# A decoder kernel's first stage, the projection of x for latent attention: by groups of four batches, or by single batches with the next group made in between

## The chip, the cores and the metric

The kernel runs on one core of one Trainium2 chip. The metric is the device time of one execution in microseconds; three timed runs of the kernel before gave 3162.03, 3165.73 and 3168.84, median 3165.73.

## The reference

A decoder of two layers on x of 16 batches by 100 tokens by 512 features: latent attention, cross attention and a sign-quantised feed-forward in layer 0, attention, cross attention and a quantised feed-forward in layer 1, each with a residual sum and a layer norm behind it. The stage in question computes, for all 1600 tokens, what the latent attention needs:

```python
cq = h_t @ Wc + bc                      # 512 -> 128
q = (cq @ Wcq + bcq)                    # 128 -> 512
qr = _rope((cq @ Wqr + bqr))            # 128 -> 256
ckv = h_t @ Wckv + bckv                 # 512 -> 128
k = (ckv @ Wck + bck)                   # 128 -> 512
kr = _rope((h_t @ Wkr + bkr))           # 512 -> 256
v = (ckv @ Wv + bv)                     # 128 -> 512
```

The rotation is not in this stage. Each token's q, qr, k, kr and v leave as one row of 16 heads x 160 values (10 KB), with a few columns of padding between.

## The kernel before

The program is written engine by engine: for each stage there is a function for SyncE (which issues all DMAs), TensorE, ScalarE, VectorE and GpSimd, and semaphores between them. A stage's functions begin by waiting until the stores of the stage before have landed (`finish`, L210). The order of each engine is the order of the code; nothing is planned by a scheduler.

Matmuls are made with parts: an operand is split into a high part (ScalarE, `copy_hi`, L160) and a low part (VectorE, `sub_lo`, L163), and `mm3` (L166) adds three products on lines L168, L169 and L170. So every operand passes ScalarE, then VectorE, before TensorE can read it.

The stage `mla_project` (L594), written m1 in the tile names, works in 4 groups of 4 batches (400 tokens). `weights` (L229) loads seven weights through two landing buffers, `raw0` and `raw1`; a load waits until the low part of the weight before it in that buffer is made. Behind them SyncE issues eight small loads (`small_load`, L571: biases broadcast over 128 partitions, two columns, the padding), then x of the first group (L376, 100 partitions x 4 x 512). Per group TensorE turns x (16 transposes, L427, through three banks), waits for all high and low parts, makes the two features cq and ckv (24 matmuls of 400 columns), waits for their high and low parts, and projects batch by batch: q, qr, k, kr, v, 24 matmuls a batch, into five banks. VectorE adds the bias to each of the five outputs (L730) while it writes them to one of two row buffers, and SyncE stores each batch's rows (L652). A row buffer is written again when its store has landed. On all engines the groups are turns of a hardware loop (`Fori`).

`load_next` (L206) issues the first two weights of the next stage, `kv_and_attend`, as soon as their landing buffers are free; here it stands behind the loop of three groups, ahead of the last four stores.

## Time and profile before

| | |
|---|---|
| median of three timed runs | 3165.73 us (3162.03 to 3168.84) |
| the profiled execution's own time | 3160.35 us |
| its span | 3158.5 us |
| TensorE busy in the span | 2777.5 us, 88% |
| VectorE, ScalarE, GpSimd busy | 2065.2, 1676.1 and 1727.2 us |
| the stage in question | 0 to 162.0 us |

The span is the time between the first and the last instruction of the profiled execution. Each engine runs its instructions in order, so a wait in one delays all behind it on that engine. The granted clock of TensorE is given as a share of 2.4 GHz: 0.50 is 1.2 GHz. In names of tiles the buffer numbers are left out, so m1_x0 is written m_x. A DMA share is the mean busy share of the core's 16 DMA engines.

### The profile page before, as it was taken

How to read it: one execution, taken by the hardware profiler on the slowest of the kernel's cores; microseconds unless marked ns; L12 is line 12 of the kernel's file. 1: busy time of each engine (PE TensorE's matmuls, PEld its weight loads, DVE VectorE, ACT ScalarE, POOL GpSimd, SP SyncE). 2: the span in 40 equal slices, each digit the busy share in tenths (PEclk: the TensorE clock that was granted, in tenths of full speed). 3: DMA queues.
4: the chain of work that ended last, by engine and by line, in shares of the span. 5: the costliest groups of instructions: out<-in, count | busy, mean ns of one | idle time of the engine just before them, and what ended most of it. 6: DMA issues, size and time to landing. Idle time of an engine off the chain costs nothing. (4 is left out here: it accounts for less than half of the span.)

```text
span 3158.5 us, 48987 instructions
## 1 busy us (share of the span) xinstructions
PE 2777.5 (88%) x16162; PEld 2495.8 (79%) x16162; DVE 2065.2 (65%) x4090; ACT 1676.1 (53%) x4247; POOL 1727.2 (55%) x2145
## 2 busy tenths in 40 slices
PE   5789999964899999998599789999999997789998
PEld 4668888754788888886499778898888886669998
DVE  3467777743687888888446547677777777774334
ACT  1056666611788888776164355666656553443222
POOL 0057777700666766666154357888888786450000
PEclk9989999966999999998799889999999998889999
DMA  3545545434343333333321221321212111542101
GB/s 122 187 132 162 154 146 160 140 96 142 106 133 101 112 114 98 106 101 105 85 82 59 81 100 54 100 79 35 89 42 86 36 51 51 173 131 92 32 27 32
DMA packets 215374, 310.74 MB, mean 98 GB/s; under 512 B 47259, under 2 KB 112895, under 8 KB 213023
## 3 DMA queue, kind: packets, MB, share of 16 engines
q1 hardware_dynamic: 215134, 307.73, 31.1%
q8 instruction: 128, 2.10, 0.3%
q14 instruction: 112, 0.91, 0.1%
HBM read 211.30 MB, written 96.37 MB: 97 GB/s over the span
## 5 line engine op out<-in xcount | busy, mean ns | idle before, releaser
L925 POOL TENSOR_TENSOR mh_quant_d<-mh_quant_a,mh_quant_d 128x512 f32<-128x512 f32 x208 | 277.9, 1336 | 17.4
L1000 ACT ACTIVATE mh_quant_d<-mh_quant_d 128x512 f32<-128x512 f32 x256 | 159.8, 624 | 109.7 <-POOL mh_quant_d L925 109.4
L919 POOL TENSOR_SCALAR mh_quant_d<-mh_quant_a 128x512 f32<-128x512 f32 x208 | 132.9, 639 | 129.1 <-DVE mh_quant_err L903 81.3
L903 DVE TENSOR_REDUCE mh_quant_err<-mh_quant_d 128x8 f32<-128x512 f32 x256 | 173.6, 678 | 39.0 <-ACT mh_quant_d L1000 37.2
L1645 PE MATMUL bank<-ga_eT,ga_v 128*128 128x400 f32 (+1 forms) x384 | 169.9, 524 | 30.4 <-DVE ga_zl L1831 30.3
L1602 PE MATMUL bank<-ga_xt,ga_wqh 128*128 128x400 f32 x512 | 177.9, 410 | 1.6 <-DVE ga_xt L164 1.6
L2342 POOL TENSOR_TENSOR fq_var<-fq_mv,eps_ln 100x1 f32<-100x1 f32 x16 | 3.7, 229 | 315.5 <-DVE fq_mv L2285 315.5
L1371 POOL TENSOR_TENSOR kv_krs<-kv_kms,minus_half 128x4 f32<-128x4 f32 x48 | 50.0, 1042 | 230.0 <-DVE kv_kms L1359 228.7
L1795 ACT ACTIVATE ga_e<-ga_e,ga_nm 100x361 f32<-100x361 f32 x256 | 152.7, 597 | 38.5 <-DVE ga_nm L1890 37.0
L958 POOL TENSOR_TENSOR ga_quant_d<-ga_quant_a,ga_quant_near 128x512 f32<-128x512 f32 x128 | 165.2, 1291 | 13.5 <-DVE ga_quant_err L903 3.0
L1791 ACT ACTIVATE ga_e<-ga_e,ga_rs 100x361 f32<-100x361 f32 x256 | 152.6, 596 | 17.9 <-DVE ga_rs L1872 17.9
L1884 DVE SCALAR_TENSOR_TENSOR ga_e<-bank,ga_qrs,ga_mask 100x361 f32<-100x361 f32 x256 | 151.1, 590 | 14.3 <-PE bank L170 13.1
L1918 POOL TENSOR_TENSOR ga_qrs<-ga_qms,minus_half 100x4 f32<-100x4 f32 x64 | 68.3, 1068 | 168.3 <-DVE ga_qms L1825 168.3
L1774 ACT ACTIVATE ga_eT<-bank 128x300 f32<-128x300 f32 x256 | 106.4, 416 | 79.0 <-PE bank L1635 78.0
L923 POOL TENSOR_SCALAR mh_quant_d<-mh_quant_d 128x512 f32<-128x512 f32 x208 | 136.9, 658 | 17.2
L921 POOL TENSOR_SCALAR mh_quant_d<-mh_quant_d 128x512 f32<-128x512 f32 x208 | 132.9, 639 | 17.2
L1890 DVE TENSOR_REDUCE ga_nm<-ga_e 100x1 f32<-100x361 f32 x256 | 135.5, 529 | 6.7
L2731 ACT ACTIVATE mh_e<-mh_e,mh_nm 100x100 f32<-100x100 f32 x256 | 93.7, 367 | 86.2 <-DVE mh_nm L2846 86.2
L2302 DVE TENSOR_TENSOR fq_v<-fq_v 128x400 f32<-128x400 f32 x64 | 36.8, 575 | 136.6 <-ACT fq_v L2223 136.6
L1602 PEld LDWEIGHTS bank<-ga_xt,ga_wqh 128*128 128x128 f32 x512 | 97.4, 195 | 28.2 <-issue 2.0
L2223 ACT ACTIVATE fq_v<-bank 128x400 f32<-128x400 f32 x64 | 32.3, 505 | 163.8 <-PE bank L170 163.8
L168 PE MATMUL bank<-mh_zh,mh_woh 128*128 128x400 f32 x256 | 94.7, 370 | 25.6 <-DVE mh_acc L2805 16.5
(442 smaller groups left out, 10467.6 us busy)
## 6 DMA issues: line engine op xcount, KB each, us to landing
keys_turned<-kv_kt SPq DMA_DIRECT2D x16, 1448.0 KB
ga_kt<-keys_turned SPq DMA_DIRECT2D x64, 362.0 KB, 2.9
ga_xt<-x_turned SPq DMA_DIRECT2D x48, 400.0 KB, 4.9
mh_xt<-x_turned SPq DMA_DIRECT2D x48, 400.0 KB, 4.7
qkv<-m_rows SPq DMA_DIRECT2D x16, 1000.0 KB
kv_rows<-qkv SPq DMA_DIRECT2D x50, 320.0 KB, 3.3
raw<-x SPq DMA_DIRECT2D x64, 200.0 KB
kv_ctx<-in_ctx SPq DMA_DIRECT2D x32, 256.0 KB
```

The costliest lines, as they stand in the source:

```text
L903: nc.vector.tensor_reduce(self.of(self.err, i)[:, s, :], self.error(i, s), AX, ALU.add).then_inc(self.summed.sem, 1)
L919: nc.gpsimd.tensor_scalar(e, a[:], 1.0 / SHRINKS[s], MAGIC, ALU.mult, ALU.add).then_inc(made.sem, 1)
L923: nc.gpsimd.tensor_scalar(e, e, -MAGIC, SHRINKS[s], ALU.add, ALU.mult).then_inc(made.sem, 1)
L925: nc.gpsimd.tensor_tensor(e, a[:], e, ALU.subtract).then_inc(self.diff.sem, 1)
L958: nc.gpsimd.tensor_tensor(self.d[s % 2][:], a[:], near[:], ALU.subtract).then_inc(self.diff.sem, 1)
L1000: nc.scalar.activation(self.error(i, s), self.error(i, s), ACT.Square).then_inc(self.squared.sem, 1)
L1602: last = nc.tensor.matmul(ps, wq[c // 2][:, k, w_], xt[:, k, c % 2, :], start=n == 0, stop=n == 11, skip_group_check=True)
L1645: last = nc.tensor.matmul(z_bank[:, 0:N], v[m % 3][0:kk, c, :], eT[m % 2][0:kk, c, :], start=c == 0, stop=c == 2, skip_group_check=True)
L1791: nc.scalar.activation(E[o % 4][:, 0:S2], E[o % 4][:, 0:S2], ACT.Copy, scale=rs[o % 4][:])\
L1795: nc.scalar.activation(E[n % 4][:, 0:S2], E[n % 4][:, 0:S2], ACT.Exp, bias=nm[n % 4][:], accum_out=sm[n % 4][:]).then_inc(exped.sem, 1)
L1884: nc.vector.scalar_tensor_tensor(out=E[n % 4][:, 0:S2], in0=score_bank[n % 2][0:S, 0:S2], scalar=qrs[g % 2][:, hh, j:j + 1], in1=small["ma ...
L1890: nc.vector.tensor_reduce(nm[n % 4][:], E[n % 4][:, 0:S2], AX, ALU.max, negate=True).then_inc(maxed.sem, 1)
```

## The change

The stage is written anew as straight code, without loops. x is loaded by batches (100 partitions x 512) into four buffers; x0 and x1 are the first two DMAs of the program, ahead of Wc and Wckv, x2 and x3 come next, then the other weights. All seven weights have places of their own in the two landing buffers, so no load waits for another; they are split in four pieces instead of seven. The biases are loaded on 100 partitions, those of qr and kr as one tile behind the small loads.

TensorE turns one batch into one bank (4 transposes), two banks in all. Behind the projections of batches 0 and 1 of a group it turns two batches each of the next group, and behind that of batch 2 it makes the next group's features; batch 3 comes last. xh, xl, ch and cl are doubled. kr goes into the second half of qr's bank, so a batch has four outputs in four banks, and four adds. There are four row buffers. GpSimd writes the padding, VectorE did before. The next stage's two weights are issued ahead of the last two stores; before, ahead of the last four. In `weights` and in the cross attention the wait of a load for its landing buffer is now on the last reader that was noted instead of on a numbered one.

```diff
...
     def mla_project():
         ph, ctx, G = "m1", ExitStack(), 4
...
+        N, BG, XR, RR = G * S, B // G, 4, 4
+        quarter = lambda n: raw[n // 4][:, n % 4 * 512:(n % 4 + 1) * 512]
...
+        four = lambda a: a.rearrange("p (k n) -> p k n", k=KC)
+        landing = [[(four(quarter(0)), kview(t["L0_attn_Wc"])), (four(quarter(1)), kview(t["L0_attn_Wckv"]))],
+                   [(quarter(2), t["L0_attn_Wcq"]), (quarter(3)[:, 0:256], t["L0_attn_Wqr"])],
+                   [(quarter(4), t["L0_attn_Wck"]), (quarter(5), t["L0_attn_Wv"])],
+                   [(four(raw[1][:, 1024:2048]), kview(t["L0_attn_Wkr"]))]]
+        landed = [raw[0][:, 0:1024].rearrange("p (c k n) -> p c k n", c=2, k=KC), raw[0][:, 1024:1792],
+                  raw[1][:, 0:1024], four(raw[1][:, 1024:2048])]
+        parted = [wc, wq, wkv, wkr]
+        NW = len(parted)
         small, small_load, small_wait = small_loads(ph, ctx, [
...
+            ("pads", [S, 2, 2, PAD], F32, t["row_pads"].rearrange("n t s c -> t n s c")),
+            ("bcq", [S, 512], F32, row(t["L0_attn_bcq"], S)),
+            ("bck", [S, 512], F32, row(t["L0_attn_bck"], S)),
+            ("bv", [S, 512], F32, row(t["L0_attn_bv"], S))])
+        brr = sb(f"{ph}_brr", [S, 2, 256], F32, ctx)
+        x = [sb(f"{ph}_x{n}", [S, D], F32, ctx) for n in range(XR)]
+        xh, xl = ([sb(f"{ph}_x{s}{n}", [P, KC, N], F32R, ctx) for n in range(2)] for s in "hl")
+        ch, cl = ([sb(f"{ph}_c{s}{n}", [P, 2, N], F32R, ctx) for n in range(2)] for s in "hl")
+        rows = [sb(f"{ph}_rows{n}", [S, H, ROW], F32, ctx) for n in range(RR)]
+        x_bank, c_bank, out_bank = bank[0:2], bank[2:4], bank[4:8]
...
+        for slot in range(RAWS):
+            raw_read[slot].append((w_lo.sem, w_lo.upto(NW - 1)))
...
+        def turned_after(b_):
+            g, j = divmod(b_, G)
+            if g + 1 == BG:
+                return []
+            return [4 * (g + 1) + 2 * j, 4 * (g + 1) + 2 * j + 1] if j < 2 else []
+        def features_after(b_):
+            g, j = divmod(b_, G)
+            return g + 1 if j == 2 and g + 1 < BG else None
         def do_sp():
...
+            def load_x(e):
+                sp.dma_start(x[e % XR][:], rows_of(x0, e)).then_inc(x_in[e % XR].sem, 16)
+            def load_weight(n):
+                for to, src in landing[n]:
+                    sp.dma_start(to, src).then_inc(w_in[n].sem, 16)
+            load_x(0)
+            load_x(1)
+            load_weight(0)
+            load_x(2)
+            load_x(3)
+            for n in range(1, NW):
+                load_weight(n)
             small_load()
...
+            for n, name in enumerate(("L0_attn_bqr", "L0_attn_bkr")):
+                sp.dma_start(brr[:, n, :], row(t[name], S)).then_inc(brr_in.sem, 16)
+            for e in range(XR, 2 * XR):
+                since(sp, x_turned, e - XR)
+                load_x(e)
+            for b_ in range(B):
+                for e in turned_after(b_):
+                    if e + XR < B:
+                        sp.wait_ge(x_turned.sem, x_turned.upto(e))
+                        load_x(e + XR)
+                if b_ == B - 2:
+                    load_next()
+                since(sp, biased, NO * b_ + NO - 1)
+                if b_ < RR:
+                    sp.wait_ge(padded.sem, padded.upto(2 * b_ + 1))
+                sp.dma_start(qkv.rearrange("(b t) d -> b t d", t=S)[b_, :, :], rows[b_ % RR][:].rearrange("p h d -> p (h d)"))\
+                    .then_inc(rows_out[b_ % RR].sem, 16)
         def do_pe():
...
+            def turn_x(e):
+                pe.wait_ge(x_in[e % XR].sem, x_in[e % XR].upto(e // XR))
+                since(pe, x_lo, e - 2)
+                for k in range(KC):
+                    last = nc.tensor.transpose(x_bank[e % 2][:, k * S:(k + 1) * S], x[e % XR][:, k * P:(k + 1) * P], ident[0:S, 0:S])
+                last.then_inc(x_turned.sem, 1)
+            def features(g):
+                since(pe, x_lo, G * g + G - 1)
+                for n in range(2):
+                    if g == 0:
+                        pe.wait_ge(w_lo.sem, w_lo.upto(0))
+                    since(pe, c_lo, 2 * (g - 1) + n)
                     for k in range(KC):
...
+                        last = mm3(c_bank[n][:, 0:N], wc[0][:, n, k, :], wc[1][:, n, k, :], xh[g % 2][:, k, :], xl[g % 2][:, k, :],
+                                   k == 0, k == KC - 1)
+                    last.then_inc(c_full.sem, 1)
+            def project(b_):
+                g, j = divmod(b_, G)
+                c_h, c_l = (lambda n: ch[g % 2][:, n, cols(j)]), (lambda n: cl[g % 2][:, n, cols(j)])
...
+                def ready(o, w_):
+                    if b_ == 0:
+                        pe.wait_ge(w_lo.sem, w_lo.upto(w_))
+                    since(pe, biased, NO * (b_ - 1) + o)
+                pe.wait_ge(c_lo.sem, c_lo.upto(2 * g))
+                ready(0, 1)
+                out(0, 0, wq, 0, 512).then_inc(out_full.sem, 1)
+                pe.wait_ge(c_lo.sem, c_lo.upto(2 * g + 1))
+                ready(1, 2)
+                out(1, 1, wkv, 0, 512).then_inc(out_full.sem, 1)
+                ready(2, 3)
+                out(2, 0, wq, 512, 256)
+                for k in range(KC):
+                    last = mm3(out_bank[2][0:S, 256:512], xh[g % 2][:, k, cols(j)], xl[g % 2][:, k, cols(j)],
+                               wkr[0][:, k, :], wkr[1][:, k, :], k == 0, k == KC - 1)
+                last.then_inc(out_full.sem, 1)
+                ready(3, 2)
+                out(3, 1, wkv, 512, 512).then_inc(out_full.sem, 1)
+            for e in range(G):
+                turn_x(e)
+            features(0)
+            for b_ in range(B):
+                project(b_)
+                for e in turned_after(b_):
+                    turn_x(e)
+                if features_after(b_) is not None:
+                    features(features_after(b_))
...
+            def turned_hi(e):
+                g, j = divmod(e, G)
+                act.wait_ge(x_turned.sem, x_turned.upto(e))
+                if j == 0:
+                    since(act, out_full, NO * (G * (g - 1)) - 1)
+                copy_hi(xh[g % 2][:, :, cols(j)], x_bank[e % 2][:, 0:KC * S].rearrange("p (k s) -> p k s", k=KC)).then_inc(x_hi.sem, 1)
+            def features_hi(g):
+                since(act, out_full, NO * (G * (g - 1)) - 1)
+                for n, bias in enumerate(("bc", "bckv")):
+                    act.wait_ge(c_full.sem, c_full.upto(2 * g + n))
+                    nc.scalar.activation(ch[g % 2][:, n, :], c_bank[n][:, 0:N], ACT.Identity, bias=small[bias][:]).then_inc(c_hi.sem, 1)
+            weight_hi(0)
+            for e in range(G):
+                turned_hi(e)
+            for n in range(1, NW):
+                weight_hi(n)
             small_wait(act)
...
+            features_hi(0)
+            for b_ in range(B):
+                for e in turned_after(b_):
+                    turned_hi(e)
+                if features_after(b_) is not None:
+                    features_hi(features_after(b_))
...
+            def add_biases(b_):
+                r = rows[b_ % RR]
+                heads = lambda a: a.rearrange("p (h d) -> p h d", h=H)
+                since(dve, rows_out[b_ % RR], b_ // RR - 1)
+                for o, at, bias in ((0, 0, "bcq"), (1, K_AT, "bck"), (2, DH, None), (3, V_AT, "bv")):
+                    dve.wait_ge(out_full.sem, out_full.upto(NO * b_ + o))
+                    if bias is not None:
+                        nc.vector.tensor_tensor(r[:, :, at:at + DH], heads(out_bank[o][0:S, :]), heads(small[bias][:]), ALU.add)\
+                            .then_inc(biased.sem, 1)
+                    else:
+                        both = r[:, :, 0:2 * K_AT].rearrange("p h (c d) -> p c h d", c=2)[:, :, :, at:at + DR]
+                        nc.vector.tensor_tensor(both, out_bank[o][0:S, :].rearrange("p (c h d) -> p c h d", c=2, h=H),
+                                                brr[:].rearrange("p c (h d) -> p c h d", h=H), ALU.add).then_inc(biased.sem, 1)
+            weight_lo(0)
+            for e in range(G):
+                turned_lo(e)
+            for n in range(1, NW):
+                weight_lo(n)
             small_wait(dve)
...
+            features_lo(0)
+            dve.wait_ge(brr_in.sem, brr_in.upto(0))
+            for b_ in range(B):
+                add_biases(b_)
+                for e in turned_after(b_):
+                    turned_lo(e)
...
+                    nc.gpsimd.tensor_copy(rows[n][:, :, at:at + PAD],
+                                          small["pads"][:, n % 2, side, :].unsqueeze(1).broadcast_to([S, H, PAD])).then_inc(padded.sem, 1)
+        finish(ph, dict(sp=do_sp, pe=do_pe, act=do_act, dve=do_dve, pool=do_pool),
+               [(s_.sem, s_.upto(s_.events - 1)) for s_ in rows_out])
+        for s_ in (w_in + x_in + rows_out + [w_hi, w_lo, brr_in, x_turned, x_hi, x_lo, c_full, c_hi, c_lo, out_full, biased, padded]):
+            s_.hand_back()
         ctx.close()
```

TensorE, the start of a group before (`m1_x` is x, `bank0` to `bank2` its banks, `xh` and `xl` the parts of turned x):

```order
L427 MATMUL bank0<-ident,m1_x 128x100 x4
L425 REGISTER_ALU
L427 MATMUL bank1<-ident,m1_x 128x100 x4
L425 REGISTER_ALU
L427 MATMUL bank2<-ident,m1_x 128x100 x4
L425 REGISTER_ALU
L427 MATMUL bank0<-ident,m1_x 128x100 x4
L457 REGISTER_ALU
L675 REGISTER_ALU
L168 MATMUL bank1<-m1_xh,m1_wch 128x400
L169 MATMUL bank1<-m1_xl,m1_wch 128x400
L170 MATMUL bank1<-m1_xh,m1_wcl 128x400
```

All four blocks of transposes, then the features, then the projections; nothing of another group stands between.

TensorE after, the end of the second batch of group 0 (bank7, v) and the start of the third (bank4, q):

```order
L168 MATMUL bank7<-m1_wkvh,m1_ch0 100x512
L169 MATMUL bank7<-m1_wkvl,m1_ch0 100x512
L170 MATMUL bank7<-m1_wkvh,m1_cl0 100x512
L699 MATMUL bank0<-ident,m1_x2 128x100 x4
L699 MATMUL bank1<-ident,m1_x3 128x100 x4
L168 MATMUL bank4<-m1_wqh,m1_ch0 100x512
L169 MATMUL bank4<-m1_wql,m1_ch0 100x512
L170 MATMUL bank4<-m1_wqh,m1_cl0 100x512
L168 MATMUL bank5<-m1_wkvh,m1_ch0 100x512
```

The transposes of x2 and x3, of group 1, now stand between two projections of group 0.

TensorE after, the end of the third batch and what follows it (`m1_xh1` belongs to group 1):

```order
L168 MATMUL bank7<-m1_wkvh,m1_ch0 100x512
L169 MATMUL bank7<-m1_wkvl,m1_ch0 100x512
L170 MATMUL bank7<-m1_wkvh,m1_cl0 100x512
L168 MATMUL bank2<-m1_xh1,m1_wch 128x400
L169 MATMUL bank2<-m1_xl1,m1_wch 128x400
L170 MATMUL bank2<-m1_xh1,m1_wcl 128x400
L168 MATMUL bank2<-m1_xh1,m1_wch 128x400
```

The features of group 1 moved ahead of the projection of the last batch of group 0.

SyncE before, the end of the start:

```order
L571 DMA m1_bcq<-in_L0_attn_bcq 128x512
L571 DMA m1_bqr<-in_L0_attn_bqr 128x256
L571 DMA m1_bck<-in_L0_attn_bck 128x512
L571 DMA m1_bkr<-in_L0_attn_bkr 128x256
L571 DMA m1_bv<-in_L0_attn_bv 128x512
L571 DMA m1_pads<-in_row_pads 100x2x32
L376 DMA m1_x<-in_x 100x4x512
L655 UNCONDITIONAL_BRANCH
```

SyncE after, the first loads of the program:

```order
L662 DMA m1_x0<-in_x 100x512
L662 DMA m1_x1<-in_x 100x512
L666 DMA raw0<-in_L0_attn_Wc 128x4x128
L666 DMA raw0<-in_L0_attn_Wckv 128x4x128
L662 DMA m1_x2<-in_x 100x512
L662 DMA m1_x3<-in_x 100x512
L666 DMA raw0<-in_L0_attn_Wcq 128x512
L666 DMA raw0<-in_L0_attn_Wqr 128x256
L666 DMA raw1<-in_L0_attn_Wck 128x512
L666 DMA raw1<-in_L0_attn_Wv 128x512
L666 DMA raw1<-in_L0_attn_Wkr 128x4x256
L572 DMA m1_bc<-in_L0_attn_bc 128x1
```

x moved from behind the small loads to the front of the queue.

SyncE before, the next stage's weights and the last stores:

```order
L655 REGISTER_ALU
L655 COMPARE_AND_BRANCH
L260 DMA raw1<-in_L0_xattn_Wk 128x4x512
L260 DMA raw0<-in_L0_xattn_Wv 128x4x512
L652 DMA qkv<-m1_rows0 100x2560
L652 DMA qkv<-m1_rows1 100x2560
L652 DMA qkv<-m1_rows0 100x2560
L652 DMA qkv<-m1_rows1 100x2560
L1073 DMA kv_ctx0<-in_ctx_2048 128x512
```

SyncE after, the same place:

```order
L691 DMA qkv<-m1_rows0 100x2560
L691 DMA qkv<-m1_rows1 100x2560
L261 DMA raw0<-in_L0_xattn_Wk 128x4x512
L261 DMA raw1<-in_L0_xattn_Wv 128x4x512
L691 DMA qkv<-m1_rows2 100x2560
L691 DMA qkv<-m1_rows3 100x2560
L1173 DMA kv_ctx0<-in_ctx_2048 128x512
```

The two weights moved from ahead of the last four stores to ahead of the last two.

## Rows read from the trace of the kernel before

**Rows 1.** timeline of SyncE's queue, end of the stage (start us, busy us, engine, line, operation).
```profile
124.05 1.26 SPq L260 DMA_DIRECT2D raw<-in_L_xattn_Wk  x1
125.37 1.78 SPq L260 DMA_DIRECT2D raw<-in_L_xattn_Wv  x1
...
162.01 0.84 SPq L1073 DMA_DIRECT2D kv_ctx<-in_ctx  x2
```

**Rows 2.** busy time by stretch (us:us, length, each engine's busy us and instructions, granted clock, DMA share, GB/s).
```profile
0.00:29.60 29.60, 0.00 (x0) 0.00 (x0) 5.78 (x11) 5.68 (x8) 0.81 (x9) 1.00 0.48 130
29.60:162.00 132.40, 97.91 (x544) 83.41 (x544) 56.38 (x104) 12.19 (x24) 0.00 (x0) 0.91 0.46 158
```

**Rows 3.** timeline of the start (start us, busy us, engine, line, operation, idle before and releaser).
```profile
0.73 0.46 SPq L260 DMA_DIRECT2D raw<-in_L_attn_Wc  x1
3.74 1.28 ACT L161 ACT_TABLE_LOAD   x1 [3.74 <-DMA raw<-in_L_attn_Wc]
...
14.47 0.38 SPq L260 DMA_DIRECT2D raw<-in_L_attn_Wkr  x1
18.94 14.25 SPq L376 DMA_DIRECT2D m_x<-in_x  x2
25.87 0.90 DVE L713 COPY m_rows<-m_pads 100x256 f32<-100x256 f32 x4 [5.21 <-DMA m_pads<-in_row_pads]
29.64 3.06 PE L427 MATMUL bank<-ident,m_x 100*128 100x100 f32 x16 [29.64 <-DMA m_x<-in_x]
```

**Rows 4.** timeline of TensorE, first group and start of the second.
```profile
35.14 0.54 PE L168 MATMUL bank<-m_xh,m_wch 128*128 128x400 f32 x1
35.47 0.54 PE L169 MATMUL bank<-m_xl,m_wch 128*128 128x400 f32 x1
...
40.20 0.34 PE L169 MATMUL bank<-m_xl,m_wckvh 128*128 128x400 f32 x1
40.38 0.34 PE L170 MATMUL bank<-m_xh,m_wckvl 128*128 128x400 f32 x1
42.16 0.48 PE L168 MATMUL bank<-m_wqh,m_cqh 128*100 128x512 f32 x1 [1.44 <-DVE m_ckvl L720]
...
46.09 0.39 PE L168 MATMUL bank<-m_wqh,m_cqh 128*100 128x512 f32 x1
...
49.95 0.39 PE L168 MATMUL bank<-m_wqh,m_cqh 128*100 128x512 f32 x1
...
59.42 1.19 PE L427 MATMUL bank<-ident,m_x 100*128 100x100 f32 x12
63.17 0.93 PE L427 MATMUL bank<-ident,m_x 100*128 100x100 f32 x4 [2.56 <-DVE m_xl L164]
```

**Rows 5.** waits from 29 to 162 us (who for whom: us in total, times, longest).
```profile
DVE m_rows L730 <- DMA qkv<-m_rows: 23.6, 8, 3.9
```

**Rows 6.** timelines of SyncE's queue and VectorE, first group's stores.
```profile
47.21 15.20 SPq L652 DMA_DIRECT2D qkv<-m_rows  x4
54.74 0.69 DVE L730 TENSOR_TENSOR m_rows<-bank,m_bcq 100x512 f32<-100x512 f32 x1 [3.89 <-DMA qkv<-m_rows]
...
59.35 0.69 DVE L730 TENSOR_TENSOR m_rows<-bank,m_bcq 100x512 f32<-100x512 f32 x1 [2.07 <-DMA qkv<-m_rows]
```

**Rows 7.** short stretches (columns as in Rows 2).
```profile
52.00:54.00 2.00, 1.95 (x14) 1.44 (x12) 0.00 (x0) 0.00 (x0) 0.00 (x0) 1.00 0.60 210
63.00:64.00 1.00, 0.83 (x4) 0.62 (x4) 1.00 (x3) 0.00 (x0) 0.00 (x0) 0.50 0.61 184
70.00:71.00 1.00, 1.00 (x7) 1.00 (x7) 0.63 (x1) 0.27 (x1) 0.00 (x0) 1.00 0.63 240
126.00:128.00 2.00, 1.23 (x4) 1.22 (x5) 0.58 (x1) 0.04 (x1) 0.00 (x0) 0.50 0.97 330
```

More of the change, by code:

```diff
@@ L253, in load @@
         def load(part):
-            for src, cols, dsts, slot, use, *_ in part:
-                if use:
-                    sp.wait_ge(*raw_read[slot][use - 1])
+            for src, cols, dsts, slot, use, *_, before in part:
+                if before is not None:
+                    sp.wait_ge(*before)
                 dst = raw[slot][:, 0:cols]
@@ L628, in mla_project @@
-        keys = [("x", k) for k in range(KC)] + ["cq", "ckv"]
-        g = Group(ph, ctx, G, x0, x0, x0, False, keys, bank[0:3], added=False)
-        b = g.bank
-        ob = Bank(sem(f"{ph}_out_full"), sem(f"{ph}_out_free"), [(o, j) for j in range(G) for o in outs], bank[3:8])
-        c_h = {n: sb(f"{ph}_{n}h", [P, N], F32R, ctx) for n in ("cq", "ckv")}
-        c_l = {n: sb(f"{ph}_{n}l", [P, N], F32R, ctx) for n in ("cq", "ckv")}
-        c_bias = {"cq": small["bc"], "ckv": small["bckv"]}
-        c_hi = Marks(sem(f"{ph}_c_hi"), ["cq", "ckv"])
@@ new lines, in mla_project @@
+        xh, xl = ([sb(f"{ph}_x{s}{n}", [P, KC, N], F32R, ctx) for n in range(2)] for s in "hl")
+        ch, cl = ([sb(f"{ph}_c{s}{n}", [P, 2, N], F32R, ctx) for n in range(2)] for s in "hl")
+        rows = [sb(f"{ph}_rows{n}", [S, H, ROW], F32, ctx) for n in range(RR)]
+        x_bank, c_bank, out_bank = bank[0:2], bank[2:4], bank[4:8]
+        NO = len(out_bank)
+        w_in = [Signal(f"{ph}_w_in{n}", 1, 16 * len(landing[n])) for n in range(NW)]
+        w_hi, w_lo = (Signal(f"{ph}_{c}", NW) for c in ("w_hi", "w_lo"))
@@ new lines, in do_dve, with weight_lo, turned_lo, features_lo @@
+        def do_dve():
+            def weight_lo(n):
+                dve.wait_ge(w_hi.sem, w_hi.upto(n))
+                sub_lo(parted[n][1][:], landed[n], parted[n][0][:]).then_inc(w_lo.sem, 1)
+            def turned_lo(e):
+                g, j = divmod(e, G)
+                dve.wait_ge(x_hi.sem, x_hi.upto(e))
+                sub_lo(xl[g % 2][:, :, cols(j)], x_bank[e % 2][:, 0:KC * S].rearrange("p (k s) -> p k s", k=KC),
+                       xh[g % 2][:, :, cols(j)]).then_inc(x_lo.sem, 1)
+            def features_lo(g):
+                for n, bias in enumerate(("bc", "bckv")):
+                    dve.wait_ge(c_hi.sem, c_hi.upto(2 * g + n))
+                    nc.vector.scalar_tensor_tensor(out=cl[g % 2][:, n, :], in0=c_bank[n][:, 0:N], scalar=small[bias][:],
+                                                   in1=f32(ch[g % 2][:, n, :]), op0=ALU.add, op1=ALU.subtract).then_inc(c_lo.sem, 1)
+            def add_biases(b_):
[16 more added lines that the diff above has]
+                weight_lo(n)
+            small_wait(dve)
+            features_lo(0)
[4 more added lines that the diff above has]
+                    turned_lo(e)
+                if features_after(b_) is not None:
+                    features_lo(features_after(b_))
```

142 lines of the change are left out of this document (28 added, 114 removed).

## The prediction

> **What bounds the kernel now.** I read the busy time by stretches first. The change touches one stage, the projection of x for the latent attention, which is everything up to 162.0 us, where the next stage's first load is issued [rows 1]. In the first 29.6 us TensorE does nothing; in the 132.4 us behind it, it is busy 97.9 us and VectorE 56.4 us [rows 2]. No engine is the limit there; waits are.
>
> The timeline of the start comes next. The first weight is asked for at 0.73 us, the last (Wkr) only at 14.47, because each load waits for its half of the landing buffers. x is asked for at 18.94, behind eight small loads (the last of these lands by 25.87), and TensorE starts at 29.64 us with "DMA m_x" as releaser [rows 3]. x is the last thing loaded and the first thing needed.
>
> Then TensorE's own timeline. Projection of one batch takes 49.95 - 46.09 = 3.86 us. Between the groups the chain turn, high part, low part, features, bias, projection is serial: the transposes of the second group start at 59.42, are held at 63.17 for the low parts, and the first group's features were followed by a hole until 42.16 [rows 4]. VectorE waits 23.6 us in 8 waits for stores of the rows, since there are two row buffers [rows 5]. A store asked for at 47.21 (the row merges the group's four) frees its buffer at 54.74 (7.5 us); the store behind it frees the other at 59.35, 4.6 us later [rows 6].
>
> What the DMA engines did while stores alone ran: share 0.60, 210 GB/s; with half-clock TensorE and a store 0.61 and 184; with the 128-row weights under way 0.97 and 330 GB/s [rows 7]. 0.61 of 16 is ten engines. The Trainium skill, "DMA: Bandwidth & Descriptors", section "Why a DMA increments its semaphore by 16 and not by 1", says that a transfer's slowest dimension sets the number of engines and that 100 partitions give 10; the trace agrees. It speaks against this change: x by batches and the biases on 100 partitions (128 before) all go on those ten, and so do the stores.
>
> **The parts.** *Start.* Now the queue holds, in order, x0, x1, Wc, Wckv, x2, x3, the other weights, the small loads. Of the way from asking to landing 2.2 us is no transfer: Wc takes 3.74 - 0.73 = 3.0 us, and 0.26 MB at 330 GB/s is 0.8 [rows 3, 7]. For 100-row transfers I take about 230 GB/s, an estimate from 1.02 MB in 4.6 us (222) and the 210 above. Four x are 0.82 MB, 3.6 us; Wc and Wckv 1.6 us: they have landed at 0.7 + 2.2 + 1.8 (two x) + 1.6 = 6.3. The table load of 1.28 us [rows 3] and the high part of 1024 columns (about 1.1, an estimate at twice a 512-column one) end at 8.7. Four batches then go through two banks, ScalarE and VectorE by turns, with the low part of the weights (1.2 us) ahead of them on VectorE: low parts end at 10.6, 11.2, 12.5 and 13.3. Features of group 0 are 24 matmuls, a dozen at the half-clock step of 0.33 us (35.14 to 35.47) and a dozen at 0.18 (40.20 to 40.38) [rows 4]: 6.2 to 6.7 us, ending at 20. That cold half is there before as well.
>
> The second branch of the start is the small loads, for which both ScalarE and VectorE wait before the features' biases. Before, Wkr is asked for at 14.47 and x begins to be used at 29.64 [rows 3]: 15.2 less 2.2 is 13.0 us of queue, of which 0.52 MB and 1.05 MB of 128-row loads at 330 are 4.8 and x is 3.6; the rest, 4.6 us, is the price of the tiny pieces (pads, the two columns) and of the broadcasts. Now: x 3.6, all weights 1.97 MB 6.0, three biases 0.61 MB 2.7, tiny pieces 4.6, together 16.9, so landed at 0.7 + 2.2 + 16.9 = 19.8. High and low part of the first feature are 1.3 us more: the first projection starts at **21** (18 if the tiny pieces cost 1.6, 25 if the whole queue runs a quarter slower). Before it was 42.16 [rows 4]: 21 us less.
>
> *Between the groups.* TensorE now has 16 x 3.86 = 61.8 us of projection, three more sets of features at 24 x 0.18 = 4.4, and 12 batches' transposes, 12 in 1.19 us, so 0.4 each [rows 4], in all 61.8 + 13.1 + 4.8 = 79.7 us from the first projection on. Everything that the next features need is made one or two batches earlier: transposes behind batches 0 and 1 of a group, features behind batch 2, the features' high and low parts beside batch 3 (3.86 us against 1.3). VectorE per batch has four adds (about 2.5 us, from 0.69 each [rows 6]), one low part and a half feature, under 3.5 us of 5. The two-bank hand-over costs TensorE nothing as the older two low parts are a batch old. The clock: now TensorE is granted half in the stretch 63 to 64 us, after the hole behind the transposes, and full again by 70 to 71 [rows 7]; without holes it should stay at 2.4 GHz. The skill's page "TensorE: Matmul & The Clock Gate", section "The HAM clock gate (the "warmup" mystery)", makes idleness, not load, the cause of the half clock; by that rule the steady part is all warm, and the sum needs no cold term beyond group 0. If the wait for the small loads opens a hole of about 2.6 us ahead of the first projection, the trace's own example says some 6 us at half clock, 3 us lost; I keep that in the range.
>
> *Stores.* With four row buffers VectorE's 23.6 us go. What is late next is the ten DMA engines. A batch is ready about 1.2 us behind its last matmul (wait, add of 0.69, issue), and then its store needs 4.6 us of them, a batch of x 0.9 to 1.0. In groups 0 and 1 that is 4 x 4.6 + 4 x 1.0 = 22.4 us against TensorE's 15.4 + 4.4 + 1.6 = 21.4, in group 2 18.4 against 21.4: level. Batch 11, the last with features ahead of it, is ready 12 x 3.86 + 13.1 + 4.8 + 0.4 (the wait for the second feature at the start) + 1.2 = 65.8 us after the first projection began and finds the queue empty. Batches 12 to 15 come every 3.86 us and need 4.6 each, and the next stage's two weights (2.1 MB, both waiting only for this stage's low parts) are now asked for between stores 13 and 14; before, they are asked for at 124.05, ahead of a projection that gives the queue nothing to store for 15 us [rows 1]. 2.1 MB at 330 GB/s is 6.4 us in front of the last two stores. So: 65.8 + 0.7 (from asking to the first byte) + 5 x 4.6 + 6.4 + 2.1 (last byte to semaphore) = 98.0 us after the first projection, while TensorE is done at about 80. The stage ends at 21 + 98 = **119** instead of 162, a gain of 43 us.
>
> *The rest.* The pads move to GpSimd, idle here, behind the same small loads; they are needed by the first store, 5 us later; nothing (up to 2 us if its copies take a microsecond each). Two adds of 16 columns a head become one of 32; the same data, nothing. The loops become straight code; the bound is a few waits for code, of which no row here shows one inside a stage: 0, at most 5. The other stages get the two landing buffers in swapped order; I find no load that waits longer: 0, between -3 and 3.
>
> *Sum.* The profiled execution took 3160.35 us around a span of 3158.5; less 43 is 3117.4. The three timed runs have a median of 3165.73, 5.4 above it, so the forecast for a median is 3117.4 + 5.4 = 3122.8, rounded **3122**.
>
> **The rivals.** *TensorE sets the end.* If the six engines that the stores leave idle take the weights and the other ten are not held up, or if the stores go faster together than 4.6, then the end is the last batch alone: 80 + 1.2 + 7.6 = 89 after the first projection, at 110; gain 52, 3114. For it: 0.97 share with weights and a store together. Against it: each engine has its own sixteenth of the weights in the same queue.
>
> *A late start.* The small loads land at 24 and TensorE runs the first batches at half clock: 25 + 3 + 98 = 126 to 128; gain 34 to 36, 3131. For it: the small loads took 4.6 us that bytes don't explain. Against: two bias loads fewer in that wait.
>
> *The holes stay.* The change doesn't do what it says for the group boundary, say because a feature's low part or a turned x is still late; then only the start is gained, 21 us: 3145. Against it: the order of instructions gives each a batch of cover.
>
> *Slower.* One mechanism: dense stores and x loads slow each other on the ten engines. With the start at 25, 16 stores of s us, 8 x loads, the weights and 2.8 us of ends give 42 + 16 s; from s = 7.5 the stage ends no sooner than 162. At 8 us a store it ends at 170, 3174. For it: a lone store takes 7.5 us. Against: two in flight are 4.6 apart, and 3 us of it is latency.
>
> **How the numbers follow.** Forecast 0.60 (its own range 3115 to 3130), TensorE sets the end 0.15, late start 0.13, holes stay 0.09, slower 0.03. The range 3107 to 3138 takes the first three with their bounds and leaves out the last two, in all some 0.17. What a measurement of this kernel tells from no change is about 0.2%, 6 us. Faster by more: 0.95; the slow mechanism near its break-even counts 0.02 for the same and 0.03 for slower.
>
> **What would show it.** TensorE's first transpose before 6 us and the first 512-column projection at about 21; the clock at full from group 0 on; no wait of VectorE for the rows' store; DMA share near 0.6 throughout and near 1.0 once, at about 95 us; TensorE done near 101 and the next stage's first load near 119, with TensorE and VectorE both waiting for the store. If the next stage starts within 10 us of the last matmul, the last term is wrong; if TensorE has gaps of microseconds at group ends, the cover is. If the other stages together move by more than 5 us, the sum is wrong for a reason that I have not named.

## The result, and the profile after

The changed kernel takes 3116.74 us (median of 4 runs, 3111.62 to 3124.22) against 3165.37 for the kernel before (4 runs, 3162.03 to 3168.84): ratio 0.9847, 95% interval 0.9825 to 0.9868. The forecast was 3122, range 3107 to 3138.

| | before | after | change |
|---|---|---|---|
| profiled execution | 3160.35 | 3111.62 | -48.7 |
| first transpose of TensorE | 29.64 | 4.00 | -25.6 |
| first 512-column projection | 42.16 | 19.58 | -22.6 |
| last matmul of the stage starts | 151.55 | 99.06 | -52.5 |
| end of the stage (next stage's first load issued) | 162.01 | 116.00 | -46.0 |

The stage gives 46.0 us of the 48.7. The other 2.7 lie in the stages behind it, which the change leaves alone but for the landing buffers' order. Over the profiled executions of this study the span behind the stage's end lies between 2990.2 and 3002.3 us, so 2.7 is no effect that can be claimed. The 46.0 us of the stage are 22.6 up to the first projection and 23.4 behind it.

The end of the stage in SyncE's queue, for [rows 1]:

```profile
53.28 39.49 SPq L691 DMA_DIRECT2D qkv<-m_rows  x9
92.82 2.13 SPq L261 DMA_DIRECT2D raw<-in_L_xattn_Wk  x1
95.00 1.64 SPq L261 DMA_DIRECT2D raw<-in_L_xattn_Wv  x1
96.68 3.83 SPq L691 DMA_DIRECT2D qkv<-m_rows  x2
116.00 0.84 SPq L1173 DMA_DIRECT2D kv_ctx<-in_ctx  x2
```

The first row merges the stores of batches 5 to 13, which come at TensorE's pace. Then SyncE asks for the two weights, then for the last two stores (at 96.68 and 100.2), and for 15.5 us it issues nothing. Before, the last store was asked for at 154.3, 7.7 us ahead of the end of [rows 1].

The start, for [rows 3]:

```profile
0.73 0.76 SPq L662 DMA_DIRECT2D m_x<-in_x  x2
1.54 0.40 SPq L666 DMA_DIRECT2D raw<-in_L_attn_Wc  x1
...
4.00 1.92 PE L699 MATMUL bank<-ident,m_x 100*128 100x100 f32 x8 [4.00 <-DMA m_x<-in_x]
6.52 1.28 ACT L161 ACT_TABLE_LOAD   x1 [6.52 <-DMA raw<-in_L_attn_Wckv]
...
15.82 3.85 POOL L832 COPY m_rows<-m_pads 100x256 f32<-100x256 f32 x8 [14.35 <-DMA m_bv<-in_L_attn_bv]
```

x0 is used at 4.00. ScalarE starts when Wckv lands, at 6.52; the small loads have landed at 15.82, when GpSimd copies the padding.

TensorE's timeline, for [rows 4]; the row at 24.32 is the transposes of x4 and x5, the last one the stage's last matmul:

```profile
13.61 0.70 PE L168 MATMUL bank<-m_xh,m_wch 128*128 128x400 f32 x1 [1.20 <-DVE m_xl L164]
...
19.58 0.40 PE L168 MATMUL bank<-m_wqh,m_ch 128*100 128x512 f32 x1
...
21.09 0.47 PE L168 MATMUL bank<-m_wkvh,m_ch 128*100 128x512 f32 x1 [0.65 <-DVE m_cl L796]
...
24.32 0.85 PE L699 MATMUL bank<-ident,m_x 100*128 100x100 f32 x8
24.95 0.47 PE L168 MATMUL bank<-m_wqh,m_ch 128*100 128x512 f32 x1
...
99.06 0.39 PE L170 MATMUL bank<-m_wkvh,m_cl 128*100 128x512 f32 x1
```

The features follow the low part of x3 at 13.61, run into the first projection without a gap at 19.58, and the wait left is one of 0.65 us for the second feature. The transposes of the first two batches of group 1, 0.63 us from 24.32 to 24.95, stand between two projections.

Short stretches, for [rows 2, 7] (length, TensorE, its weight load, VectorE, ScalarE and GpSimd busy us, granted clock, DMA share, GB/s):

```profile
30.00:40.00 10.00, 10.00 (x60) 9.09 (x59) 5.61 (x10) 1.51 (x3) 0.00 (x0) 1.00 0.64 231
40.00:50.00 10.00, 10.00 (x69) 8.58 (x68) 7.26 (x12) 0.90 (x2) 0.00 (x0) 1.00 0.55 190
...
70.00:80.00 10.00, 10.00 (x65) 9.19 (x64) 5.65 (x9) 1.49 (x3) 0.00 (x0) 1.00 0.62 237
...
96.00:100.00 4.00, 3.45 (x23) 2.65 (x21) 2.84 (x5) 0.00 (x0) 0.00 (x0) 1.00 0.88 306
100.00:104.00 4.00, 0.00 (x0) 0.00 (x0) 0.18 (x1) 0.00 (x0) 0.00 (x0) 0.78 0.88 293
...
108.00:112.00 4.00, 0.00 (x0) 0.00 (x0) 0.00 (x0) 0.00 (x0) 0.00 (x0) 0.50 0.61 261
```

From 30 to 80 us TensorE is never idle and is granted 2.4 GHz throughout; the share of the DMA engines is 0.55 to 0.64, that is nine to ten of sixteen. From 96 to 104 it is 0.88, from 108 to 112 again 0.61; there TensorE has had nothing to do since 99.45 and is granted 1.2 GHz. Of VectorE's waits for stores ([rows 5], 23.6 us) none is left within the stage; the one wait of that kind is now the end itself:

```profile
DVE kv_kt L1378 <- DMA qkv<-m_rows: 15.9, 1, 15.9
```

### The profile page after: what moved, and what is told of

Read it like the earlier page. It is cut to its first block and busy times, and to the rows that moved or that the text cites. A ratio compares the mean times of both kernels' runs of the same rounds, so it can differ in the third digit from the quotient of the medians.

```text
span 3109.8 us, 48704 instructions
## 1 busy us (share of the span) xinstructions
PE 2769.8 (89%) x16162; PEld 2492.6 (80%) x16162; DVE 2064.4 (66%) x4067; ACT 1673.8 (54%) x4244; POOL 1731.5 (56%) x2153
## 5 line engine op out<-in xcount | busy, mean ns | idle before, releaser
L1984 DVE SCALAR_TENSOR_TENSOR ga_e<-bank,ga_qrs,ga_mask 100x361 f32<-100x361 f32 x256 | 151.1, 590 | 14.8 <-PE bank L170 13.3
```

## The experiments

The stages behind this one move by several us between executions, so a whole time tells little of a few us. I read each run's profile at two places: the first 512-column projection on TensorE, and the next stage's first load. Their difference is 96.4 us in the changed kernel (19.58 to 116.00), and 119.9 before. The first features begin with matmuls every 0.33 us and go on with one every 0.18 (from 17.03 in the changed kernel). How long the slow part lasts differs between executions (the features take 6.0 to 7.3 us in eleven of the runs here), which moves both places together; the difference is free of that, and it repeats: the four kernels whose edit touches only the start or nothing (changed, e6, f1, f3) give 96.2 to 96.4. Some kernels were timed once; their "median" is that one time. The kernel before, timed again beside them, had medians of 3152.68 (e2, e5, e6, e8), 3160.46 (e1, e3, e4, e7) and 3162.62 (f1 to f4), so whole times of different groups are compared only by their ratio to it.

| kernel | timed runs | median us | first projection | end of stage | difference |
|---|---|---|---|---|---|
| changed | 4 | 3116.74 | 19.58 | 116.00 | 96.4 |
| e1, weights ahead of the first store | 4 | 3113.93 | 21.02 | 112.46 | 91.4 |
| e2, weights behind the last store | 1 | 3111.48 | 19.35 | 110.58 | 91.2 |
| e3, turning and features at the group's end | 4 | 3126.02 | 20.71 | 130.14 | 109.4 |
| e4, stores of 96 and 4 rows | 4 | 3120.74 | 19.92 | 111.92 | 92.0 |
| e5, two row buffers | 1 | 3117.61 | 20.55 | 119.38 | 98.8 |
| e6, x behind the small loads | 1 | 3126.93 | 27.25 | 123.56 | 96.3 |
| e7, e1 and e4 | 5 | 3112.03 | 20.54 | 107.56 | 87.0 |
| e8, kernel before with x first | 1 | 3150.48 | 38.55 | 158.48 | 119.9 |
| f1, x0 and x1 ahead of the weight's parts | 1 | 3117.23 | 17.55 | 113.70 | 96.2 |
| f2, e7 and f1 | 5 | 3106.95 | 18.80 | 104.93 | 86.1 |
| f3, broadcasts on 128 partitions | 1 | 3112.56 | 20.03 | 116.25 | 96.2 |
| f4, only the features at the group's end | 1 | 3121.46 | 21.12 | 119.30 | 98.2 |

Theory: once TensorE runs through, the end of the stage is a queue of ten DMA engines, and the next stage's weights stand in it in front of the last two stores. Rival: the stores are slow when they are dense.

**e1, the weights ahead of the first store.**

```diff
-                if b_ == B - 2:
+                if b_ == 0:
                     load_next()
```

> The changed kernel, but the next stage's two weights are asked for ahead of the first store of rows instead of ahead of the last two. Theory (they stand in the queues of the ten engines in front of the last two stores): the stage ends 6.4 us earlier, at 109.6 instead of 116.0, median about 3110. Rival (the last stores are late because dense stores are slower than 4.6 us each): the stage ends at 115 to 116 and nothing is gained.

Measured: end at 112.46, with the first projection 1.4 us later than in the changed kernel; the difference falls by 5.0 of the expected 6.4. The whole time shows none of it: the ratio to before is 0.9855 (0.9831 to 0.9878) against the changed kernel's 0.9847. SyncE's queue shows the weights at the start of the stores; the DMA share is 0.22 from 20 to 30 us there, and 0.83 from 30 to 40 where it was 0.64:

```profile
27.02 0.40 SPq L261 DMA_DIRECT2D raw<-in_L_xattn_Wk  x1
27.46 1.39 SPq L261 DMA_DIRECT2D raw<-in_L_xattn_Wv  x1
28.97 0.37 SPq L691 DMA_DIRECT2D qkv<-m_rows  x1
...
112.46 0.85 SPq L1173 DMA_DIRECT2D kv_ctx<-in_ctx  x2
```

**e2, the weights behind the last store.**

```diff
-                if b_ == B - 2:
-                    load_next()
...
+            load_next()
```

> The changed kernel, but the next stage's two weights are asked for behind the last store. Theory (they take 6.4 us of the ten engines wherever they stand): the next stage's first load is issued at 109.6 instead of 116.0, but ScalarE's first high part of its weights starts only at 115 to 117, as before the move (116), and the whole is the same within 2 us. Rival (the tail has another cause): first load at 116 and first high part at 123, 6 us slower.

Measured: first load at 110.58 and the difference 91.2, the same as with the weights first; ScalarE's first part of the weights starts at 113.31, waiting for them, against 116.10 in the changed kernel:

```profile
100.26 2.24 SPq L261 DMA_DIRECT2D raw<-in_L_xattn_Wk  x1
102.54 2.27 SPq L261 DMA_DIRECT2D raw<-in_L_xattn_Wv  x1
110.58 0.82 SPq L1172 DMA_DIRECT2D kv_ctx<-in_ctx  x2
```

and ScalarE's timeline of the same run:

```profile
113.31 1.91 ACT L161 ACTIVATE kv_wkh<-raw 128x2048 fp32r<-128x2048 f32 x1 [32.71 <-DMA raw<-in_L_xattn_Wk]
115.78 1.91 ACT L161 ACTIVATE kv_wvh<-raw 128x2048 fp32r<-128x2048 f32 x1 [0.57 <-DMA raw<-in_L_xattn_Wv]
```

So the two loads cost the last stores about 5 us where they stand in front of them and nothing where they don't, ahead or behind. The theory holds and the rival is out for these 5 us, for the stores are as dense as before. Behind the last store the loads are not free for the next stage: ScalarE starts 2.7 us behind the stage's end instead of 0.1, and comes to its first features 9.5 us behind it (at 120.12), where it is 7.5 in the changed kernel and at most 8.5 in every other run but e7. That the weights land at 113.3 and not at 115 to 117 I had not expected; the DMA engines that no store uses were free for their share, but no run tells whether that is why.

**e4, each store as 96 and 4 rows.**

```diff
-                sp.dma_start(qkv...[b_, :, :], rows[b_ % RR][:]...).then_inc(rows_out[b_ % RR].sem, 16)
+                for a, z in ((0, 96), (96, S)):
+                    sp.dma_start(qkv...[b_, a:z, :], rows[b_ % RR][a:z]...).then_inc(rows_out[b_ % RR].sem, 16)
```

> The changed kernel, but each store of 100 rows is made as two, 96 rows and 4 rows. Theory (the store is limited by its ten engines at about 22 GB/s each): a store takes 3.2 us of the busiest engine instead of 4.6, the DMA share during stores rises from 0.62 towards 0.9, and the stage ends at about 110. Rival (225 GB/s is what writing to memory gives): share and rate stay, the stage ends at 116.

Measured: end at 111.92, the difference 4.4 less; of the theory's 6. The share rises, but not to 0.9, for the same bytes:

```profile
70.00:80.00 10.00, 10.00 (x66) 9.21 (x65) 5.95 (x10) 1.49 (x3) 0.00 (x0) 1.00 0.76 237
...
100.00:110.00 10.00, 0.00 (x0) 0.00 (x0) 0.53 (x1) 0.00 (x0) 0.00 (x0) 0.66 0.90 338
```

In the same stretch of the changed kernel it is 0.62 at 237 GB/s. That is 237 / (0.62 x 16) = 24 GB/s for a busy engine with ten of them at work, and 237 / (0.76 x 16) = 19.5 with the stores split. In the tail of the same run, with the weights under way too, it is 338 / (0.90 x 16) = 23.5. So the split store used its engines less well in the steady part, but a busy engine has no fixed rate here, and why the gain is 4.4 us and not 6 is not shown. The whole time of e4 (3120.74, ratio 0.9877, 0.9855 to 0.9900) doesn't show the gain: its profiled execution took 4.1 us less to the stage's end and 8.5 more behind it than the changed kernel's (3002.3 against 2993.8). No run ties those 8.5 us to the edit.

**e7, both.**

> The changed kernel with both: the next stage's weights ahead of the first store, and stores of 96 and 4 rows. Theory (both are one queue, and TensorE is the limit once it is clear): the stage ends about 6.5 us after the last store is asked for at 100.2, at 106.5, median 3107, ratio to before 0.982. Rival (one of the two was all): 109.6.

Measured: end at 107.56, difference 87.0, 9.4 less than in the changed kernel; the two gains add (5.0 + 4.4). The last three of the 32 part stores are issued from 97.67 to 102.0, and the stage ends 5.6 us later. In the stretch with the weights and the first stores together all sixteen engines are busy. The median is 3112.03, ratio to before 0.9843 (0.9822 to 0.9864); the changed kernel's is 0.9847, so the whole time does not show the 9.4 us (0.3%) either, and misses the expected 3107. In this profile ScalarE comes to the next stage's first features 10.0 us behind the stage's end instead of 7.5; in f2, with the same stores and weights, it is 7.9, so the edit is not known to be the cause.

```profile
30.00:40.00 10.00, 10.00 (x63) 9.07 (x61) 5.43 (x10) 2.09 (x4) 0.00 (x0) 1.00 1.01 358
```

**e3, everything of the next group at the group's end.**

```diff
-            return [4 * (g + 1) + 2 * j, 4 * (g + 1) + 2 * j + 1] if j < 2 else []
+            return [4 * (g + 1) + n for n in range(G)] if j == G - 1 else []
...
-            return g + 1 if j == 2 and g + 1 < BG else None
+            return g + 1 if j == G - 1 and g + 1 < BG else None
```

> The changed kernel, but the next group's four batches are turned and its features made behind the last batch of a group, nothing of it in between. Theory (the making in between hides the chain turn, high part, low part): each of three borders costs TensorE 3 to 4 us, and 3 more where the clock falls; the stage ends at 126, up to 135. Rival (the ten engines with the stores are the limit throughout): under 3 us later, 116 to 119.

Measured: end at 130.14, the difference 13.0 more, within 10 to 19; the ratio to before is 0.9895 (0.9868 to 0.9922) against 0.9847. TensorE's waits from 18 to 128 us:

```profile
PE bank L168 <- DVE m_xl L164: 3.6, 3, 1.2
PE bank L699 <- DVE m_xl L164: 2.9, 3, 1.0
PE bank L168 <- DVE m_cl L796: 2.6, 4, 0.7
```

and stretches at the three borders:

```profile
40.00:45.00 5.00, 3.99 (x14) 3.99 (x15) 0.96 (x2) 0.64 (x2) 0.00 (x0) 0.69 0.53 164
...
65.00:70.00 5.00, 3.64 (x22) 3.37 (x23) 1.54 (x4) 1.06 (x3) 0.00 (x0) 1.00 0.59 184
...
90.00:95.00 5.00, 3.80 (x19) 3.47 (x20) 1.33 (x3) 0.99 (x2) 0.00 (x0) 0.81 0.60 240
```

The waits are 9.1 us, 8.5 more than in the changed kernel (0.6), 2.8 for each of three borders. TensorE's last matmul starts 93.6 us after the first projection instead of 79.5, so it loses 14.1 us and 5.6 of them are no waits (1.1 of the 14.1 do not reach the stage's end). The clock is a part of the 5.6: the granted clock is 0.50 from 42 to 45 us at the first border and from 94 to 96 at the third. Over 40 to 50 us its mean is 0.69 and then 0.97, over 90 to 100 it is 0.81 and then 0.85, so 5 x 0.31 + 5 x 0.03 and 5 x 0.19 + 5 x 0.15, about 1.7 us each, are the estimate of what it costs. At the second border it stays at 1.00, although TensorE's waits there are the same (0.95, 1.20 and 0.64 us, with transposes between the first two). What the other 2 us are, is not shown.

**f4, only the features at the group's end.** The edit is the second of e3's two.

> The changed kernel, but the next group's features are made behind the last batch of a group instead of behind the third; turning stays in between. Theory (batch 3 covers the features' high and low parts): TensorE has a wait of about 1 us at each of three borders, as it has at the start, and the stage ends 2 to 3 us later counted from the first projection (99 instead of 96.4), so of the 13 us that making all of it at the group's end cost, the turning is 10. Rival (the features' parts are the larger half): 7 or more.

Measured: the difference is 98.2, 1.8 us more. TensorE's waits for the features' low parts are 2.6 us in 4 instead of 0.6 in 1, and the clock stays at 1.00 (20 to 100 us). So of e3's 13.0 us, 2 are the features alone, and 11 come with the turning of x, its parts and the clock that falls there.

**e5, two row buffers.**

```diff
-        N, BG, XR, RR = G * S, B // G, 4, 4
+        N, BG, XR, RR = G * S, B // G, 4, 2
```

> The changed kernel with two row buffers instead of four. Theory (a buffer's turn is 7.5 us of store and 3.3 of adds, so 5.4 us a batch, against 4.9 that TensorE needs on the mean and 3.86 in the last group): VectorE waits for stores again, and the stage ends 3 to 8 us later, 119 to 124. Rival (the queue is the limit at 4.6 a store anyway): 116 to 117.

Measured: end at 119.38, the difference 2.4 us more, just under the expected 3 to 8. VectorE waits 27.9 us for stores, more than before the change:

```profile
DVE m_rows L806 <- DMA qkv<-m_rows: 27.9, 12, 3.6
...
PE bank L168 <- DVE m_rows L806: 3.2, 6, 1.3
```

Most of these waits cost nothing: TensorE waits only 3.2 us for VectorE in turn. A wait of VectorE for a store counts only when TensorE then waits for VectorE. TensorE's last matmul starts 4.4 us later, counted from the first projection (83.9 against 79.5), and 2.4 of that reach the end of the stage.

**e6, x behind the small loads.**

```diff
-            load_x(0)
-            load_x(1)
-            load_weight(0)
-            load_x(2)
-            load_x(3)
-            for n in range(1, NW):
+            for n in range(NW):
                 load_weight(n)
             small_load()
...
-            for e in range(XR, 2 * XR):
+            for e in range(2 * XR):
```

> The changed kernel, but x is asked for behind the small loads, as before the change. Theory (at the start the chain from x is the last): x0 lands at about 16 instead of 4, the features of group 0 start at 21.5 instead of 13.6, the stage ends 8 us later, at 124. Rival (the small loads are the last, as the prediction had it): they land 3.6 us earlier and the stage ends no later than 118.

Measured: first transpose at 15.30, first features at 20.46, first projection at 27.25, end at 123.56; the difference is unchanged at 96.3. The order of loading alone is worth 7.6 us in the changed kernel. The small loads landed at 13.19 there, 2.6 earlier than with x ahead, and decided nothing.

**e8, the kernel before with x first.**

```diff
+            g.load_x(0)
             w["rest"]()
             small_load()
-            g.load_x(0)
```

> The kernel before, with one part of the change: x of the first group is asked for as the first load of the stage's own (behind the first two weights). Theory (TensorE waits for all low parts of the weights, and VectorE for the small loads, so x is only one of three): first transpose at about 22 to 24 instead of 29.6, first features at 29 to 31 instead of 34.0, the stage ends 3 to 6 us earlier than 162. Rival (x was the only late thing): it gains nearly all of the 21 us of the start.

Measured: first transpose at 25.16, first features at 30.05, end at 158.48, 3.5 us earlier. The time behind the first projection is the same as before to 0.1 us. The row of TensorE's first transposes names only its own sequencer. In the code they stand behind the wait for all low parts of the weights, and the last of these, Wkr's, whose load still comes fourth through its buffer, is made from 22.96 to 24.19, 1.0 us ahead of them. So x first alone is worth 3.6 us of the 22.6 that the first projection gained. No run gave the weights their own places and left x where it was in the kernel before; e6 is the nearest, and there the start still gains 14.9 (42.16 to 27.25).

VectorE and TensorE in e8's timeline:

```profile
22.96 1.23 DVE L164 TENSOR_TENSOR m_wkrl<-raw,m_wkrh 128x1024 fp32r<-128x1024 f32 x1 [4.49 <-ACT m_wkrh L161]
25.16 2.26 PE L427 MATMUL bank<-ident,m_x 100*128 100x100 f32 x12 [25.16 <-PEq L415]
...
30.05 0.69 PE L168 MATMUL bank<-m_xh,m_wch 128*128 128x400 f32 x1 [1.28 <-DVE m_xl L164]
```

**f1, the parts of x0 and x1 ahead of those of the first weight.**

```diff
-            weight_hi(0)
             for e in range(G):
+                if e == 2:
+                    weight_hi(0)
                 turned_hi(e)
```

and the same on VectorE with `weight_lo(0)` and `turned_lo(e)`.

> The changed kernel, but ScalarE and VectorE make the parts of x0 and x1 ahead of those of the first weight (Wc, Wckv), not behind. Theory (the start is one chain of x through two banks and these two engines): the features start at 11 to 11.5 us instead of 13.6, the first projection at 17.5, or up to 18.5 where the small loads (landed at 15.8) hold the first bias, and the stage ends 1 to 2 us earlier, at 114 to 115. Rival (the arrival of Wc, Wckv and x3 sets the start): features not before 13.

Measured: features at 10.97, first projection at 17.55, end at 113.70, 2.3 us earlier. The start is the chain of x through ScalarE and VectorE; the arrival of the weights is not last.

**f3, the broadcasts on 128 partitions.**

```diff
-            ("bcq", [S, 512], F32, row(t["L0_attn_bcq"], S)),
+            ("bcq", [P, 512], F32, row(t["L0_attn_bcq"], P)),
```

and the same for bck and bv.

> The changed kernel, but the three bias broadcasts behind the small loads go to 128 partitions again (on sixteen engines) instead of 100 (on ten). By the count of engines alone they land 0.3 us earlier (0.79 MB at 330 GB/s is 2.4, 0.61 at 230 is 2.7), so GpSimd's first copy of the padding starts at 15.5 to 15.8. Rival (a broadcast to 128 partitions is slow in itself, and that was the 4.6 us that bytes did not explain before): the copy starts 1 to 3 us later, at 17 to 19.

Measured: the copy starts at 18.49. In the ten runs with the start of the changed kernel or f1's it starts between 15.26 and 17.79 (15.82 in the changed kernel itself), so 18.49 is the latest of all, by 0.7; a loss of 1 to 3 us fits better than a gain of 0.3, but one run against that spread does not settle it. The first projection (20.03) stays within the spread of the others (19.35 to 21.12).

**f2, e7 and f1 together.**

> The changed kernel with stores of 96 and 4 rows, the next stage's weights ahead of the first store, and x0, x1 ahead of the first weight's parts. Theory: the stage ends at 105 to 106, from 107.6 without the last edit; whole time 10 us under the changed kernel's by the stage, about 3107, ratio to before 0.981 to 0.984. Rival (the other stages take the gain back): ratio 0.985 as for the changed kernel.

Measured: 3106.95 us (5 runs, 3105.08 to 3108.47), ratio to before 0.9826, interval 0.9808 to 0.9843; end of the stage at 104.93. That is the fastest version of this study; its interval overlaps the changed kernel's (0.9825 to 0.9868), so the whole time does not prove the gain; the stage's end, 11.1 us earlier, does not depend on the other stages. Here the small loads are the last thing at the start for once: ScalarE's first feature waits 4.5 us for them and TensorE 1.8 us for that.

```profile
ACT m_ch L768 <- DMA m_bv<-in_L_attn_bv: 4.5, 1, 4.5
...
PE bank L168 <- DVE m_cl L798: 1.8, 1, 1.8
```

## Why the prediction was right

**The start.** Forecast 21 for the first projection, measured 19.58. The chain of x came out as worked: low parts by 13.3 (the features start at 13.61), features of 6.0 us. The branch that was to decide, the small loads at 19.8, was wrong: they land at 15.8. The failed step is the carrying over of "the tiny pieces 4.6"; a queue of 16.9 us was really 15.82 - 0.7 - 2.2 = 12.9, of which bytes explain 12.3. e6 bounds it again: without x in front they land at 13.19, 10.3 us of queue for 8.7 of bytes. So the tiny pieces cost 0.6 to 1.6 by these two runs, and up to 2.6 by the latest landing of ten such starts (17.79, in f4). What the 4.6 us of the kernel before were stays open; f3 points at the broadcasts on 128 partitions but does not settle it. The miss is only 1.4 us by luck: the 21 came from a branch that was 4 us too late, and the one that decided, the end of the features, happened to stand at 20. Of the start's 22.6 us, x first is worth 7.7 in the changed kernel (e6) and 3.6 in the kernel before (e8). What the weights' own places are worth by themselves, no run tells. The prediction calls the slow matmuls of the first features half-clock ones. That reading rests on their step of 0.33 us against 0.18 alone: the row of the granted clock shows 1.00 over 10 to 20 us in the changed kernel and over 35 to 41 in the kernel before.

**Between the groups.** Right: no wait of TensorE and no half clock from 22 us on. TensorE's part from the first projection to the last matmul's end is 99.45 - 19.58 = 79.9 us, forecast 79.7. That it fits to 0.2 us is two small errors that cancel: the transposes of two batches take 0.63 us, so 3.8 in all and not 4.8, and the wait of 0.65 us for the second feature was not in this sum. e3 prices the cover at 13.0 us, with a clock term of about 1.7 us at two of three borders that I had only for a late start; f4 gives 1.8 of it to the features.

The prediction did not ask where the time behind the first projection went in the kernel before. Its TensorE took 109.8 us from there to its last matmul (42.16 to 151.94), 29.9 more than now, of which 6.5 do not show because the last stores are later now. e3 and e5 take 13.0 and 2.4 of the 23.4 us back; some 8 us are left that no run assigns. TensorE's waits for VectorE's adds are gone and may be a part of them; this is the row of the kernel before:

```profile
PE bank L168 <- DVE m_rows L730: 5.9, 4, 1.5
```

Five outputs became four in the same rewriting, and the loops went; none of this was taken back by itself.

**Stores.** The mechanism was right, the ten engines, a queue that is level until group 2, the weights in front of the last two. Difference forecast 98.0, measured 96.4. The term for the weights was 6.4 and is worth 5.0 to 5.2 (e1, e2). It was priced at the 330 GB/s of sixteen engines, 20.6 each; at the 24 GB/s that a busy engine moved with ten at work, an engine's sixteenth of 2.1 MB takes 5.5 us, an estimate that comes closer. The DMA share was to come near 1.0 once, at about 95 us; it came to 0.88, from 96 to 104. The rival "TensorE sets the end" would have given 89; e7, which clears the queue, comes to 87.0. That a row count of 96 brings more engines in shows in e4's share (0.76 against 0.62 for the same 237 GB/s). The Trainium skill, "DMA: Bandwidth & Descriptors", section "Why a DMA increments its semaphore by 16 and not by 1", gives sixteen engines for 96 partitions; the trace agrees, and adds that a busy one of them then moved less there, 19.5 GB/s against 24.

**Four row buffers.** I put VectorE's 23.6 us of waits among what goes, and they went, but e5 shows that in the changed kernel such waits are worth 2.4 us: the stage's end was not theirs.

**The rest.** GpSimd's padding, the merged adds and the straight code cost nothing that shows; there is no row with a wait for code in TensorE's stage after the start. The range was said to leave out two rivals of "some 0.17"; their own chances, 0.09 and 0.03, make 0.12. The forecast added 5.4 us from profile to median on 3117.4. Against the profiled 3111.62 the error is 5.8 us: 3.0 in this stage and 2.8 behind it, which is within what those stages vary by.

## What to carry over

When the engine that computes stops waiting, look at which transfers now meet at the end of the stage: loads for the next stage that were free in the old pauses stand in front of the last stores in the new ones, and moving one line takes 5 us off the end of the stage. Whether the whole program gains them has to be seen by itself; here its times vary by more. Count the partitions of each transfer, since the 100-row ones here all kept to about ten of the sixteen engines, and read the end of a stage rather than the whole time where the stages behind it vary by more than the effect.

## What the runs showed of the hardware

- Storing rows of 10 KB, a busy DMA engine moved 24 GB/s with ten at work (0.62 share at 237 GB/s, changed kernel, 70 to 80 us) and 19.5 with the stores split over sixteen (0.76 at 237, e4). With loads of 128 rows beside them it was 22 (358 GB/s at a share of 1.01, e7, 30 to 40 us) and 23.5 (338 at 0.90, e4, 100 to 110 us).
- The same three waits of TensorE at a group's border (0.95, 1.20 and 0.64 to 0.66 us, transposes between the first two) were followed by 1.2 GHz at the first and the third border of e3 (42 to 45 and 94 to 96 us) and left the clock at 2.4 GHz at the second. A single wait of 1.8 us in f2 left it at 2.4 GHz too.
- The small loads land at times that spread by 2.5 us between executions of the same start (15.26 to 17.79).
- GpSimd's eight copies of 100x256 take 3.85 to 4.4 us in the four runs in which VectorE makes the low part of Wkr beside them (changed kernel, e3, e4, e7) and 2.8 us in the seven in which no low part of a weight is made beside them (e1, e2, e6, f1 to f4); no run tried the cause.
